# Group convolution, channel shuffle and what follows: shuffled image laid out (half, channel) by (group, pixel)

## The reference

```python
x = x + L0(gn(x))      # 16 images, 512 channels, 32 x 32, float32
x = x + L1(gn(x))
# gn: group norm, 32 groups of 16 channels
# L0: 3x3 convolution in 8 groups of 64 channels, bias, then per group
out = out.reshape(B, G, gout, L).transpose(0, 1, 3, 2).reshape(B, G * gout, Ho, Wo)
# L1: h = relu(bn1(conv1x1(x)))            512 -> 128 channels
#     offset = conv3x3(h)                  18 channels
#     out = deform_conv3x3(h, offset)      four neighbours of each of 9 taps, bilinear
#     out = relu(bn3(conv1x1(bn2(out))))   128 -> 512 channels
```

## Time and profile before

| | |
|---|---|
| median of three runs | 1784.15 us (1783.03 to 1786.91) |
| the profiled execution | 1782.21 us |
| its span, first to last instruction | 1780.3 us |
| TensorE, VectorE, ScalarE, GpSimd busy | 91%, 79%, 54%, 67% |
| granted TensorE clock, mean | 0.974 of 2.4 GHz |
| DMA | 412.93 MB, 232 GB/s |

### The profile page before, as it was taken

How to read it: one execution, slowest core, us unless ns; L and a number is a source line. 1 busy time by engine, 2 the same in 40 slices (tenths; PEclk the granted TensorE clock), 3 DMA queues, 4 the chain that set the end, 5 groups by cost and what they waited for, 6 DMA issues and landing times.

```text
span 1780.3 us, 31909 instructions
## 1 busy us (share of the span) xinstructions
PE 1623.2 (91%) x10144; PEld 922.4 (52%) x10144; DVE 1399.9 (79%) x3450; ACT 964.5 (54%) x1475; POOL 1187.4 (67%) x1159
## 2 busy tenths in 40 slices
PE   2899999999999999999999999999999999997654
PEld 0555564555556465555646555564655556563221
DVE  4357789788888979888897978888797888877664
ACT  4664656565564656556555556656565654533212
POOL 0007777776767677677767767677776767677774
PEclk9999999999999999999999999999999999998768
DMA  7017677878787788778788777878788777777875
GB/s 227 1 49 232 203 245 255 272 233 276 210 275 237 256 261 258 245 214 284 221 261 261 257 247 219 283 216 267 244 262 259 246 257 213 227 231 221 263 223 165
DMA packets 142451, 412.93 MB, mean 232 GB/s; under 512 B 24518, under 2 KB 25030, under 8 KB 142150
## 3 DMA queue, kind: packets, MB, share of 16 engines
q0 software_dynamic: 92160, 302.06, 56.7%
q1 hardware_dynamic: 49814, 106.27, 16.0%
q10 hardware_dynamic: 304, 2.44, 0.6%
HBM read 339.37 MB, written 71.30 MB: 231 GB/s over the span
## 4 chain that ended last, share of the span: by engine, by line
PE 48%; DVE 19%; issue 12%; POOL 11%; ACT 6%; DMA 2%; DVEq 0%; ACTq 0%; POOLq 0%
PE bank L735 17%; POOL sb_rows L316 11%; PE bank L749 8%; PE bank L717 7%; DVE sb_rows L533 6%; DVE sb_split L574 4%; DVE sb_val L541 4%; PE bank L802 4%; PE bank L708 3%; PE bank L824 3%; PE bank L724 3%; ACT sb_split L392 3%; PE bank L767 2%; DVE sb_raw L589 1%; DVE sb_diff L634 1%
## 5 line engine op out<-in xcount | busy, mean ns | idle before, releaser
L316 POOL DMA_INDIRECT sb_rows<-table,sb_ridx x1152 | 1185.3, 1029 | 553.8 <-issue 454.4
L533 DVE SCALAR_TENSOR_TENSOR sb_rows<-sb_rows,sb_frac 128x256 f32<-128x256 f32 x1152 | 492.3, 479 | 106.7 <-DMA sb_rows<-table,sb_ridx 101.9
L735 PE MATMUL bank<-sb_split,sb_wg 128*128 128x512 f16 x2304 | 551.9, 385 | 17.2 <-issue 8.5
L735 PEld LDWEIGHTS bank<-sb_split,sb_wg 128*128 128x128 f16 x2304 | 219.1, 98 | 300.6 <-issue 70.9
L541 DVE SCALAR_TENSOR_TENSOR sb_val<-sb_rows,sb_frac 128x128 f32<-128x128 f32 x1152 | 328.7, 347 | 15.4 <-PE bank L708 0.2
L717 PE MATMUL bank<-sb_valT,sb_wd 128*128 128x512 f32 x576 | 322.3, 643 | 0.0
L364 ACT ACTIVATE sb_conv_sb<-bank,sb_bias 128x512 f32<-128x512 f32 x256 | 173.6, 684 | 263.5 <-PE bank L735 222.9
L346 ACT ACTIVATE sb_valT<-bank 128x512 f32<-128x512 f32 x288 | 170.9, 593 | 268.1 <-PE bank L708 267.8
L749 PE MATMUL bank<-sb_fold_sb,sb_conv_sb 128*64 128x64 f32 x4096 | 261.3, 281 | 1.7 <-ACT sb_conv_sb L364 1.6
L749 PEld LDWEIGHTS bank<-sb_fold_sb,sb_conv_sb 128*64 128x64 f32 x4096 | 244.0, 207 | 31.1 <-issue 27.9
L708 PE MATMUL bank<-sb_eye_sb,sb_val 128*128 128x128 f32 x1152 | 182.3, 282 | 67.6 <-DVE sb_val L541 53.3
(11 more groups left out here) (76 smaller groups left out, 1012.4 us busy)
## 6 DMA issues: line engine op xcount, KB each, us to landing
table<-sb_table_sb SPq DMA_DIRECT2D x144, 256.0 KB, 4.1
sb_xs<-x SPq DMA_DIRECT2D x64, 512.0 KB, 10.1
out<-sb_res SPq DMA_DIRECT2D x128, 256.0 KB, 4.0
sb_rows<-table,sb_ridx POOLq DMA_INDIRECT x1152, 4.0
sb_rows<-w_group ACTq DMA_DIRECT2D x2, 1152.0 KB, 13.9
sb_wd<-w_def SPq DMA_DIRECT2D x1, 576.0 KB
sb_w<-w_in SPq DMA_DIRECT2D x1, 256.0 KB
sb_w<-w_out SPq DMA_DIRECT2D x1, 256.0 KB
```

The costliest lines, as they stand in the source:

```text
L316: pool.indirect_dma_start(out=rows[:, (c % RING) * PER + i, :], out_offset=None, in_=tables[u % 2], in_offset=bass.IndirectOffsetOnAxis(ap ...
L533: op = nc.vector.scalar_tensor_tensor(r[:, 0:2 * CH], r[:, 2 * CH:4 * CH], frac[:, parity, half * PER + i, k, 0:1], r[:, 0:2 * CH], ALU.mu ...
L735: op = nc.tensor.matmul(pair_ps[half][:, :], wg[:, g, k, :], plane(split1[:, g, :], ky + half * HROWS, kx, HROWS), start=k == 0, stop=k == ...
```

## The change

The shuffled image gets a layout of its own. Partition 64 * half + c holds new channel c's pixels of that half; along the partition stand eight groups of 512 pixels. The image is kept in two forms: `xc` (one buffer, channels on partitions) for the first norm, and `xl` (three buffers, new layout) to which the shuffle is added and from which all later stages read. Both are loaded from HBM.

- Group convolution: high and low weights are 64 columns each and accumulate in the same place; two groups of a quarter go to the two halves of the output partitions. 18 matmuls of 64 columns stand where nine of 128 stood, at the same slots. The fold is gone, and ScalarE evicts once per quarter and half (`part == 1`), in the order of the new pixels, to `conv_sb`.
- Shuffle: four transposes of 128 x 128 for each of the eight pieces.
- Statistics per group and half: two aggregates and two products for each of the four; `halves` instead of `blocks` for their mean.
- Input convolution: for each group and half a matmul over 64 partitions; `scale_w1` scales eight pieces. `w_in` is loaded for both halves of the partitions.
- Output: `mid` has both halves; `out_conv(g)` makes 64 channels of both halves with two matmuls of 64 columns. All eight stand in slots 9 to 13, their relus in 10 to 13, two residual adds each in slots 11 to 14, and the stores by pairs of groups. `res` holds four groups, so `relu_out` of groups 4 and 6 waits for the store of groups 0, 1 and 2, 3 of the same image.
- Loads: `xc` quarter by quarter behind `norm1_done`, `xl` by pairs of groups in slots 11 to 14 behind the store of a pair.
- `differences` makes the differences first and the low part last.
- The loop holds six steps instead of four.

```diff
-        xs = sb("xs", [128, XBUFS, QUADS, PIX], f32)
+        xc = sb("xc", [128, QUADS, PIX], f32)
+        xl = sb("xl", [128, XBUFS, GROUPS, HALF], f32)
...
+        CONV_FIRST = {3: 7, 4: 8, 5: 9, 6: 10, 7: 11, 8: 13, 9: 14, 12: 1, 13: 3}
+        CONV_THEN = {2: 6, 7: 12, 9: 15, 11: 0, 12: 2, 16: 4, 17: 5}
...
+        OUT_END = {9: 0, 10: 2, 11: 4, 12: 6}
+        OUT_MID = {10: 1, 11: 3, 12: 5, 13: 7}
+        RELU_FIRST = {10: 0, 11: 2, 12: 4, 13: 6}
+        RELU_THEN = {10: 1, 11: 3, 12: 5, 13: 7}
+        RESIDUAL = {11: 0, 12: 1, 13: 2, 14: 3}
...
+                    if tail and s in RESIDUAL:
+                        pair = RESIDUAL[s]
+
+                        sp.wait_ge(sum_done, count(GROUPS, t - 1, 2 * pair + 2))
+                        for half in (0, 1):
+                            dst = out[bass.ds(t - 1, 1), pair, :, half * HALF:(half + 1) * HALF]
+                            first = 2 * pair % QUADS
+                            sp.dma_start(dst.rearrange("a (e c) n -> (a c) e n", e=2),
+                                         res[64 * half:64 * half + 64, first:first + 2, :])\
+                              .then_inc(stored[pair % 2], 16)
+                    if a1 and a2 and s in RESIDUAL:
+                        pair = RESIDUAL[s]
+
+                        sp.wait_ge(mid_done, count(2 * QUADS, nxt, 2 * pair + 2))
+                        load_shuffled(pair)
...
-            def relu_out(image, half, q):
-                act.wait_ge(out_done, count(2 * QUADS, image, half * QUADS + q + 1))
-                act.wait_ge(stored[q], count(32, image, 16 * half))
-                nc.scalar.activation(res[:, q, :], out_ps[:, :], ACT.Relu, bias=bn_t[:, 2 + q:3 + q],
-                                     scale=bn_s[:, 2 + q:3 + q]).then_inc(relu_done, 1)
-
-            def conv_to_sbuf(image, g, half):
-                act.wait_ge(conv_done, count(2 * GROUPS, image, 2 * g + half + 1))
-
-                act.wait_ge(shuf_done, count(2 * QUADS, image, 2 * ((g - 3) // 2) + 2 if g >= 3 else 0))
-                nc.scalar.activation(conv_sb[:, g % 3, half * HALF:(half + 1) * HALF], pair_ps[half][:, :],
-                                     ACT.Identity, bias=bias0[:, g:g + 1]).then_inc(conv_out, 1)
+            def relu_out(image, g):
+                act.wait_ge(out_done, count(GROUPS, image, g + 1))
+                if g % 2 == 0:
+                    act.wait_ge(stored[g // 2 % 2], count(64, image, 32 * (g // 4)))
+                nc.scalar.activation(res[:, g % QUADS, :], out_ps[:, :], ACT.Relu, bias=bn_t[:, 2 + g:3 + g],
+                                     scale=bn_s[:, 2 + g:3 + g]).then_inc(relu_done, 1)
+
+            def conv_to_sbuf(image, n):
+                q, half, part = n // 4, n // 2 % 2, n % 2
+                if part == 0:
+                    return
+                act.wait_ge(conv_done, count(2 * QUADS, image, 2 * q + half + 1))
+
+                act.wait_ge(shuf_done, count(2 * QUADS, image, 2 * q - 2))
+                by_place = conv_sb[:, q % 2, :].rearrange("p (j h c) -> p c h j", h=2, j=COLS // 2)
+                nc.scalar.activation(by_place[:, half * (GIN // 2):(half + 1) * (GIN // 2)],
+                                     pair_ps[half][:, :].rearrange("p (c h j) -> p c h j", h=2, j=COLS // 2),
+                                     ACT.Identity, bias=bias0[:, q:q + 1]).then_inc(conv_out, 1)
 
...
-            def out_conv(image, half, q):
-                if q == 0:
-                    pe.wait_ge(d_out, count(2, image, half + 1))
-                pe.wait_ge(relu_done, count(2 * QUADS, image, half * QUADS + q))
-                nc.tensor.matmul(out_ps[:, :], w2[:, q * 128:(q + 1) * 128], mid[:, :], start=True, stop=True)\
-                  .then_inc(out_done, 1)
-
-            def group_conv(image, g, half):
-                pe.wait_ge(w_low, 1)
-                pe.wait_ge(low1_done, count(2 * QUADS, image, g + 1))
-                pe.wait_ge(conv_out, count(2 * GROUPS, image, 2 * g + half - 1))
-                if g == 2:
-                    pe.wait_ge(h_done, count(2, image - 1, half + 1))
+            def out_conv(image, g):
+                if g == 0:
+                    pe.wait_ge(d_out, count(2, image, 2))
+                pe.wait_ge(relu_done, count(GROUPS, image, g))
+                for half in (0, 1):
+                    op = nc.tensor.matmul(out_ps[64 * half:64 * half + 64, :], w2[:, g * GIN:(g + 1) * GIN],
+                                          mid[:, half, :], start=True, stop=True)
+                op.then_inc(out_done, 1)
+
+            def group_conv(image, n):
+                q, half, part = n // 4, n // 2 % 2, n % 2
+                if part == 0:
+                    pe.wait_ge(w_low, 1)
+                    pe.wait_ge(low1_done, count(2 * QUADS, image, 2 * q + 2))
+                    pe.wait_ge(conv_out, count(2 * QUADS, image, 2 * q + half - 1))
+                    if q == 1:
+                        pe.wait_ge(h_done, count(2, image - 1, half + 1))
                 for k in range(TAPS):
                     ky, kx = divmod(k, 3)
-                    op = nc.tensor.matmul(pair_ps[half][:, :], wg[:, g, k, :],
-                                          plane(split1[:, g, :], ky + half * HROWS, kx, HROWS),
-                                          start=k == 0, stop=k == TAPS - 1)
-                op.then_inc(conv_done, 1)
-
-            def shuffle(image, q, half):
-
-                pe.wait_ge(conv_out, count(2 * GROUPS, image, 4 * q + 4))
-                pe.wait_ge(mid_done, count(2 * QUADS, image, 2 * q + half - 1))
-                if q == 1 and half == 0:
+                    for e in (0, 1):
+                        op = nc.tensor.matmul(pair_ps[half][64 * e:64 * e + 64, :],
+                                              wg[:, 2 * q + e, k, part * GIN:(part + 1) * GIN],
+                                              plane(split1[:, 2 * q + e, :], ky + half * HROWS, kx, HROWS),
+                                              start=part == k == 0, stop=part == 1 and k == TAPS - 1)
+                if part == 1:
+                    op.then_inc(conv_done, 1)
+
+            def shuffle(image, q, part):
+
+                pe.wait_ge(conv_out, count(2 * QUADS, image, 2 * q + 2))
+                pe.wait_ge(mid_done, count(2 * QUADS, image, 2 * q + part - 1))
+                if q == 1 and part == 0:
                     pe.wait_ge(tile_out, count(TILES, image - 1, TILES))
-                for jj in range(COLS // 2):
-                    for e in (0, 1):
-                        j = half * (COLS // 2) + jj
-                        op = nc.tensor.matmul(
-                            shuf_ps[half][64 * e:64 * e + 64, jj * GIN:(jj + 1) * GIN],
-                            conv_sb[:, (2 * q + e) % 3, j:j + COLS * (GIN - 1) + 1:COLS], fold_sb[:, :],
-                            start=True, stop=True)
+                dst = shuf_ps[part].rearrange("p (e j o) -> p j e o", e=2, o=GIN)
+                for jj in range(COLS // 4):
+                    j = part * (COLS // 4) + jj
+                    op = nc.tensor.transpose(dst[:, jj], conv_sb[:, q % 2, j * 128:(j + 1) * 128], eye_sb[:, :])
...
+                        for half in (0, 1):
+                            if g == 0 and a1:
+                                pe.wait_ge(conv_out, count(2 * QUADS, new, 1 + half))
+                            elif g == 0:
+                                pe.wait_ge(conv_out, count(2 * QUADS, nxt, 2 * QUADS - 1 + half))
+                            p = slice(64 * half, 64 * half + 64)
+                            op = nc.tensor.matmul(pair_ps[half][:, :], w1_norm[p, g * CH:(g + 1) * CH],
+                                                  xl[p, (u + 1) % XBUFS, g, :], start=g == 0, stop=g == GROUPS - 1)
+                            if g == GROUPS - 1:
+                                op.then_inc(in_done, 1)
```

250 lines of the change are left out of this document (124 added, 126 removed).

## The result

| | before | changed |
|---|---|---|
| median of 4 runs | 1785.34 us (1783.03 to 1786.91) | 1859.34 us (1858.14 to 1865.09) |
| ratio | | 1.0422, 95% interval 1.0396 to 1.0448 |
| profiled execution, span | 1782.2 us, 1780.3 | 1865.1 us, 1863.3 |
| first gathering issued | 135.8 | 130.5 |
| last gathering to the end of the span | 20.4 | 38.7 |

The change costs 74 us. It was forecast at 1793 (1746 to 1845): the sign of the likeliest case was right, the time lies 66 us above it and outside the range. TensorE sheds some of its work, less than reckoned, and it does not help.

A forecast was written before the change was run, and what follows sets the result against it. It took TensorE up to VectorE's slot 10, then a chain of VectorE, ScalarE and TensorE, to bound a step, GpSimd's gathers close behind. 1780.3+7-8+10 = 1789.3, +1.9+1.9 = 1793 us; range 1746 to 1845.

The forecast's parts named there:

- likeliest case: TensorE's relief is eaten by the gathers and a new store wait: slower, 1793 us, 1775 to 1813; 39%.
- A: From the end of VectorE's slot 0 to its slot 10: 47.9 us falls to 45.0, set by GpSimd's gathers.
- Column and row pairs: Narrow matmul pairs cost like wide ones: group convolution unchanged, output piece 0.86 us, input convolution 3.54 us a slot.
- rival of 8%: Row halves of the input convolution don't pair in slots 14 and 15: +5.3 us a step, 1867 us; 8%.
- B: From VectorE's slot 10 to the add of shuffle (0,0): grows by 3.4 to 40.0 us, with a store wait before relu(4).
- first rival: The store wait before relu(4) is covered: step 1.4 to 3.2 us less than forecast, total 1748 to 1773 us; 31%.
- The tail of B: From the slot 14 copy's end to the add: transposes 0.55, shift 0.8, input convolution 3.54, shuffle 0.6 us.
- C: Rest of the step from the add of shuffle (0,0), unbroken VectorE work: keeps 17.35 us.
- Start: Before the steady steps: six shuffles there give -9 us, the doubled constants cost +1.
- End: Behind the last gather: four more output convolutions cost +8 us and a store wait 2.
- third rival: TensorE falls to 1.2 GHz around out_conv(5), slots 11 and 12: 1.7 to 4 us a step, 1817 to 1849; 18%.
- second rival: All of TensorE's relief arrives: the step falls to the gathers' 95.3 us and the total to about 1694; 4%.

The follow-up runs named there:

- shift_late: In-place residual kernel, with a PSUM bank each for six last-step output pieces and the shift product behind input convolution and first shuffled piece: 1.0031 of before, 1789.84 us.
- inplace_3: Changed kernel with the residual summed in xl, ReLUs waiting for no store, xl loads a slot later: 1.0079 of before, 1799.79 us; earlier on another chip 0.9807.
- after_ref: The changed kernel unaltered, measured once more as reference for the experiments: 1.0376 of before, 1851.97 us.
- before_ref: The kernel before the change, unaltered, measured once more as reference: 1785.37 us.

## Why the prediction was wrong, point by point

- **A, forecast 45.0: right.** The means are 44.6 and 44.3. GpSimd goes from 849.21 to 928.44 with no stop over 0.31 us, that is right through A, and VectorE waits for its gatherings. Of TensorE's 9.4 us of relief 3.5 arrive. But TensorE is not the freed engine of the forecast: it is busy through all of A, with work that used to fall behind it, such as the first output piece (891.54).
- **TensorE's busy time, forecast near 1450 us and 80%: wrong, 1580.2 and 85%.** The shuffle's group gave what was reckoned, 180.6 us of 190:

```profile
L749 PE MATMUL bank<-sb_fold_sb,sb_conv_sb 128*64 128x64 f32 x4096 | 261.3, 281 | 1.7 <-ACT sb_conv_sb L364 1.6
```

```profile
L786 PE MATMUL bank<-sb_eye_sb,sb_conv_sb 128*128 128x128 f32 x512 | 80.7, 281 | 5.9 <-ACT sb_conv_sb L386 5.9
```

  Every other group grew: the group convolution by 20.4 us, the output convolution by 20.2, the input convolution and the shift product by 16.5 each, the transposes of `val` by 10.3. By groups the sum falls by 81 us and on the page, which counts overlapping ends once, by 43. The forecast had taken the narrow forms as equal to the wide ones and left out the clock and the shift product.
- **Transposes for folding matmuls: right.** Four take 0.60 to 0.66 us for 2.04.
- **Column and row pairs: right.** 18 narrow matmuls take 2.17 us with 2.10 to the next start, against 2.16 and 1.99: the change of shape costs some 0.1 a chunk, the side on which the Trainium skill's rule on a change of tiling mode (TensorEngine Tiling (Array Packing), Key Properties) had put it. An output piece holds TensorE 0.91 us (905.61-904.70), 0.86 forecast. Sixteen row-half matmuls take 3.65 in the chain against 3.54 for eight wide ones. The rival of 8% (row halves don't pair) falls.
- **B, forecast 40.0, measured 45.3: wrong, and here lies most of the error.** B grows by 9.2 us at the mean (36.6 to 45.8) where the sum had 3.4. The step that failed is "relu(4) ends at 18.8. TensorE then does out_conv(5) ... to 26.8". relu(4) itself was right (18.1 forecast, 17.8 measured), and so was the store that it waits for. But the same wait stands before relu(6). The prediction names it, as evidence against the first rival, and gives it no term. The store of the second pair is issued at 19.4, lands 10 us later, and holds relu(6) until 29.5 in this step (27.9 at the median), so that the copy of slot 14 ends at 38.5 (37.9 at the median) and not at 34.5. Without the store waits B is 40.2, with a quick landing 44.2, with the xl loads in the queue 45.2; with the slow input convolutions taken out, 39.4, 42.6 and 44.7.
- **The tail of B, forecast 5.5 us from the copy's end to the add, measured 6.8 here and 8.5 at the median:** two terms. The shift product has twice the matmuls, eight groups instead of four pairs, and takes 1.76 for 0.8. The prediction doubled scale_w1 and the statistics and forgot this one. And the input convolution takes 3.54 as forecast only with the clock at 2.4 GHz; in 7 of 13 steps it falls, and the tail has 1.7 us more. shift_late confirms both: B loses 2.5, which is 1.76 and the 0.8 a step that the clock cost inplace_3.
- **That 40.2 without any store wait equals the forecast of 40.0 with one is chance.** The missing 1.0 us of the shift product and 0.8 us a step of slow input convolution made up for most of the 2.1 us of the wait for relu(4).
- **xl loads beside stores, taken at nothing, up to 1 us a step: too low.** B falls by 1.0 without them, but with the clock's share taken out by 2.1.
- **Scattered eviction, taken at nothing: at most 0.4 of B,** 0.47 us each.
- **C, 17.35: right to the hundredth.**
- **Start, forecast -8: measured -5.3.** I have not looked for the rest.
- **End, forecast +10, measured +18.3:** the four pieces more behind the last gathering were right, the clock was missed. In after_ref, another execution of the same kernel, the end takes 32.6 us against 21.7 of before_ref, +10.9, and there seven of the eight pieces run at 2.4 GHz, or near it:

```profile
1826.00 1.08 PE L755 MATMUL bank<-sb_mid,sb_w 128*64 128x512 f32 x4 [0.87 <-ACT sb_mid L368]
1827.95 1.08 PE L755 MATMUL bank<-sb_mid,sb_w 128*64 128x512 f32 x4 [0.88 <-ACT sb_res L375]
...
1840.15 1.98 PE L755 MATMUL bank<-sb_mid,sb_w 128*64 128x512 f32 x4 [0.87 <-ACT sb_res L375]
```

  So 6 us of the end hang on which of its two clocks TensorE has there, and this differs between executions. The prediction used the clock in its third rival and not where TensorE surely idles between pieces.
- **The third rival, a fall of the clock in B (18%, 1.7 to 4 us a step):** it happens, at two places. At the place that the rival names, out_conv(5) takes 1.97 and the convolution behind it 2.92 in the step shown, after TensorE idled for 2.61 us:

```profile
910.96 1.97 PE L755 MATMUL bank<-sb_mid,sb_w 128*64 128x512 f32 x4 [2.61 <-ACT sb_res L375]
912.72 2.92 PE L770 MATMUL bank<-sb_split,sb_wg 128*64 128x512 f16 x18
```

  This one costs nothing here, because ScalarE waits until 921.8 for the store anyway, and it goes when that wait goes. The other place no rival names: the input convolution behind the shift product, 1.0 us a step in the mean, and that is on the path. The first rival (wait covered, 31%) had the second wait as a remark only, and it is that wait that is exposed; the second rival (4%) is ruled out by A.
- **The range.** It had no case in which the second wait was exposed. Its upper end rested on the clock. In the first rival a landing of 4.3 us takes 1.1 us off the wait (5.4-4.3), not 1.4, which moves nothing.

The sum with the terms as measured: A 44.6, B 45.8, C 17.3 give 107.7 a step, 5.3 more than 102.4 of before; fourteen times 5.3 is 74, -5.3 at the start, +18.3 at the end: 1867 for a span of 1863.3.

## What to carry to other kernels

When a buffer's reuse turns a store into something that an engine waits for, list every reuse of that buffer in a step and give each one its own term: here the second wait of a ring of two stood with the whole chain behind it and lasted 8.10 us, the first 1.95. Summing in place, in the operand that the load brought, takes such a wait away and moves it to the queue that loads, so look next at what is queued there. Serial work at the end of a program is to be priced at both clocks of TensorE, and is shortened by giving it the banks that lie idle there. One step is not the steady state: count over all steps how often the clock falls on the path before two runs are compared, or a gain of 2 us looks like 1.

## What the runs showed of the hardware that I had not expected

TensorE's clock falls to 1.2 GHz in the midst of nearly unbroken work. In the slow step shown behind the table TensorE is busy 8.00 of 8.00 us from 1144 to 1152 and the granted clock there is 0.79; ahead of the fall lie a pause of 0.75 us, four transposes and 1.83 us of fp32 matmuls of one column. The step cut up at the start has a pause of 1.04 us and the same 1.83 us and no fall, so what decides it stays open. In `before`, with half as many such matmuls at that place, no step of 13 has it, and in the three runs with the product moved away the input convolution is slow in none of 39 steps.

On two chips TensorE stood still, or crawled, for up to 12 us at a time, with no releaser in the rows, and the kernel before took 2243.59 and 2245.00 us instead of 1785. One such place, timeline of TensorE in run inplace:

```profile
932.10 1.30 PE L772 MATMUL bank<-sb_split,sb_wg 128*64 128x512 f16 x10
933.74 1.07 PE L772 MATMUL bank<-sb_split,sb_wg 128*64 128x512 f16 x4 [0.34 <-issue]
935.14 1.10 PE L772 MATMUL bank<-sb_split,sb_wg 128*64 128x512 f16 x4 [0.33 <-issue]
939.47 1.09 PE L740 MATMUL bank<-sb_eye_sb,sb_val 128*128 128x128 f32 x4 [3.23 <-issue]
```

Four matmuls need 1.4 us, then nothing for 3.2, while GpSimd issues one gathering behind the other. 18 take 2.17 us otherwise, in the same profile too. The same kernel has none of this in run inplace_3, on another chip. Steps are 126 to 138 us in run inplace instead of 102. What holds TensorE in these places the rows don't show, and it stays open; a comparison is worth something only with the kernel before on the same chip.

A write of 512 columns in an order scattered over the free dimension costs ScalarE 1157 ns instead of 684 to 686.
